# Gathers of source ids and edge keys moved from the setup into the rows' stage, and the stage before layer 1 dissolved into layer 1's first tiles

## The chip, the cores and the metric

The kernel runs on one NeuronCore of a Trainium2 chip. The metric is device time in microseconds (us) of one execution; lower is better. The core has five engines that run in order, each with its own queue, and that wait for one another through semaphores: PE (TensorE, matrix products and transposes), DVE (VectorE), ACT (ScalarE), POOL (GpSimd, which also issues the indirect DMAs) and SP (SyncE, which here only issues DMAs).

## The reference

One layer of a graph network with attention over 6250 nodes of 256 features and 200,000 edges (dst is sorted).

```
xn = layernorm(x)
A  = normalized adjacency with self loops: norm(e) = dinv[src]*dinv[dst], dinv = 1/sqrt(degree)
gnn = relu(A (relu(A (xn W1) + b1) W2) + b2)
q, k, v = split(xn W_qkv + b_qkv); q, k minus their row mean; q2 = q*q, k2 = k*k
k2 = l2norm_over_nodes(k2 / (rowsum(k2) + 1e-7)); q2 = l2norm_over_columns(q2 / (rowsum(q2) + 1e-7))
mix = (v + q2 (k2^T v) / sqrt(N)) W_mo + b_mo
x1 = x + gnn + mix
out = x1 + slice_attention(layernorm(x1))      (64 slices, 8 heads)
```

## The kernel before, in words

The nodes are cut into T = 49 tiles of 128 rows. The program is a sequence of stages; each is a block in which every engine has its own list of work, and a block ends with a barrier of all engines. The stages around the change are:

1. **The setup.** It finds where each run of dst begins, counts degrees, prepares weights, and makes the edge keys. A window is two nodes; there are G = 7 groups of 112 partitions with WPS = 4 windows each, so 28 gathers. POOL issues 28 indirect DMAs (L307), each of which brings 128 source ids for each of 112 windows. DVE splits all ids at once into a low part (L425, L426) and a tile number (L428 to L431), over 3584 elements per partition. PE transposes the 56 blocks (L488) and ACT copies them as 14 groups into key_lo and key_hi (L516). SP stores the degrees to DRAM and loads them back turned (L271, L273); PE turns them, DVE copies them to degT (L434) and computes the flag (L437). A branch on that flag (`nc.values_load`, `nc.If(general == 1)`) follows; it isn't taken with these inputs.
2. **A block for dinv:** ACT takes a root (L616), DVE a reciprocal and two scalings (L621 to L624).
3. **The rows' stage.** It runs over 49 tiles with rings of 4 buffers. In its iteration t, PE does project(t) (L772 and four passes of L774), turn(t+1) (two transposes, L763) and gather(t-2) (k2 sums L782, then two transposes of q2, L789). DVE does norm(t+1) (L699 to L706), stats(t+2) (L691, L694), over_norm(t-2) (L731 to L737), over_sums(t-1) (L721 to L725) and halves(t+1) (L711). ACT does norms(t-2), std(t+2), keep(t+1), squares(t) and turned(t-3). POOL adds one tile (L821). SP loads x and stores the turned tiles.
4. **The stage between** (L886 and on). kx, the sums that the rows' stage leaves in PSUM, is copied (L918) and turned (L966), multiplied by wvo (L972) and scaled to mkv (L954, L958). Beside it runs a chain that finds the largest entries: two DVE reductions (L919, L920), an ACT square (L907), a partition_all_reduce on POOL (L903), an ACT root (L911) and eight DVE steps (L931 to L948), which give the scales of layer 1.
5. A second `nc.If(general == 1)`, whose body (sum_edges) is long and isn't run.
6. **Layer 1.** POOL writes two iotas (L1238, L1239). DVE makes one-hot matrices from the keys (hots, L1277) in 8 batches per tile, with a ring of 4 batches. PE multiplies them into adjacency blocks (build, L1321, 64 per tile), ACT copies these to `at` (store, L1379), POOL adds the self loops (L1249), and PE aggregates (L1332). Tile t+1 is built while tile t is aggregated. The iteration t = -1 only builds. relu(t-1) on ACT uses the scale dsc.

## Time and profile before

| what | us |
|---|---|
| timed executions (3) | 2064.79, 2066.60, 2067.97; median 2066.6 |
| span of the profiled execution | 2066.3 |
| PE busy | 1886.4 (91%) |
| DVE busy | 1177.8 (57%) |
| ACT busy | 850.7 (41%) |
| POOL busy | 301.8 (15%) |

The profiled execution's own time is its span, 2066.3 us. The busy shares are means over stages with different limits: from layer 1 on PE is full, while in the first sixth of the span the limit changes from stage to stage. So the parts below are read by stage, from the timeline (start, duration, engine, line, operation) and from windows of time.

### The profile page before, as it was taken

What the parts mean: (1) busy time and instruction counts of PE and PEld (TensorE: products, weight loads), DVE (VectorE), ACT (ScalarE), POOL (GpSimd) and SP (SyncE); (2) the same over time, 40 slices, a digit from 0 to 9 for tenths busy, and PEclk for the clock granted to TensorE, in tenths of its full rate; (3) what the DMA queues carried; (4) which work ended last, traced back from release to release, by engine and by line L of the source; (5) the groups of instructions that cost most, each with busy time, mean ns of one, the idle gap of its engine ahead of it and who ended that gap; (6) DMA issues with size and microseconds to landing.
All of it is one profiled execution on the core that took longest, in us unless ns stands there. A gap on an engine that the chain in (4) does not pass through costs nothing. (4 is left out here: it accounts for less than half of the span.)

```text
span 2066.3 us, 45220 instructions
## 1 busy us (share of the span) xinstructions
PE 1886.4 (91%) x18840; PEld 1417.3 (69%) x18840; DVE 1177.8 (57%) x2715; ACT 850.7 (41%) x1948; POOL 301.8 (15%) x418
## 2 busy tenths in 40 slices
PE   3069994999999999999979999999999999999598
PEld 3035552555555555555549999999999999999476
DVE  6369985666666666666623555555555555555322
ACT  2157772665656666566531222232222322322100
POOL 3502121000000000000020111111111111111033
PEclk7569996999999999999999999999999999999699
DMA  3113331232222223232335444444444444442087
GB/s 95 32 36 112 113 106 42 95 126 101 119 109 111 117 103 125 95 125 94 126 115 184 145 144 141 141 141 141 141 141 141 141 144 145 144 144 96 13 265 233
DMA packets 92701, 252.13 MB, mean 122 GB/s; under 512 B 14142, under 2 KB 59346, under 8 KB 79938
## 3 DMA queue, kind: packets, MB, share of 16 engines
q1 hardware_dynamic: 69225, 218.83, 29.7%
q10 hardware_dynamic: 21096, 25.65, 3.5%
q0 software_dynamic: 2176, 4.75, 0.9%
q8 instruction: 150, 2.46, 0.5%
q14 instruction: 54, 0.44, 0.1%
HBM read 131.99 MB, written 118.02 MB: 121 GB/s over the span
## 5 line engine op out<-in xcount | busy, mean ns | idle before, releaser
L1332 PE MATMUL ps<-hs,at 128*128 128x512 f16 x2401 | 667.8, 378 | 3.3 <-POOL at L1249 3.3
L1530 PE MATMUL ps<-at,big 128*128 128x128 f16 x9604 | 577.0, 219 | 6.5 <-DMA at<-at_scratch 6.5
L1530 PEld LDWEIGHTS ps<-at,big 128*128 128x128 f16 x9604 | 556.0, 98 | 34.2 <-issue 8.0
L1379 ACT CAST at<-ps 128x392 f16<-128x392 f32 x784 | 375.3, 486 | 302.3 <-PE ps L1321 286.2
L1321 PE MATMUL ps<-big 128*128 128x98 f16 x3136 | 472.3, 209 | 15.2 <-DVE big L1277 15.2
L1321 PEld LDWEIGHTS ps<-big 128*128 128x128 f16 x3136 | 298.3, 98 | 149.9 <-issue 14.8
L1332 PEld LDWEIGHTS ps<-hs,at 128*128 128x128 f16 x2401 | 229.8, 97 | 151.7 <-POOL at L1249 3.5
L1277 DVE TENSOR_TENSOR big<-big,key_lo 128x1024 f16<-128x1024 f16 x392 | 268.4, 685 | 0.0
L1277 DVE TENSOR_TENSOR big<-big,key_hi 128x784 f16<-128x784 f16 x392 | 219.1, 559 | 15.4 <-POOL big L1239 10.4
L1644 DVE SCALAR_TENSOR_TENSOR big<-ps,small,blogb 128x512 f32<-128x512 f32 x49 | 36.8, 751 | 230.9 <-PE ps L1566 230.9
L1747 POOL TENSOR_TENSOR key_lo<-key_lo,big 128x512 f32<-128x512 f32 (+1 forms) x49 | 61.9, 1263 | 706.6 <-ACT big L1705 706.6
L1288 DVE TENSOR_TENSOR big<-ps,big 128x256 f32<-128x256 f32 x49 | 20.8, 425 | 201.6 <-ACT big L1387 201.6
L1249 POOL TENSOR_TENSOR at<-at,ident 128x120 f16<-128x120 f16 x98 | 31.9, 336 | 655.5 <-ACT at L1379 655.5
L1693 ACT ACTIVATE big<-big,eps 128x1 f32<-128x1 f32 x49 | 14.5, 296 | 224.2 <-DVE big L1629 224.2
L1695 ACT CAST big<-ps 128x512 f16<-128x512 f32 x49 | 28.7, 585 | 170.9 <-PE ps L1557 170.9
L774 PE MATMUL ps<-at,big 128*128 128x512 f32 (+1 forms) x196 | 98.6, 626 | 0.0
L1022 PE MATMUL ps<-hs 128*128 128x256 f32 (+1 forms) x392 | 90.7, 391 | 8.6 <-DMA hs<-x_scratch 8.4
L1022 PEld LDWEIGHTS ps<-hs 128*128 128x128 f32 (+1 forms) x392 | 75.0, 195 | 24.6 <-DMA hs<-x_scratch 14.2
L1697 ACT ACTIVATE big<-big 128x512 f32<-128x512 f32 x49 | 30.8, 629 | 146.9 <-DVE big L1650 146.9
L488 PE MATMUL ps<-ident,big 112*128 112x112 f32 x56 | 10.3, 373 | 88.7 <-DVE big L426 84.3
L1615 DVE SCALAR_TENSOR_TENSOR big<-ps,dun,key_hi 128x256 f32<-128x256 f32 x49 | 23.7, 484 | 106.5 <-PE ps L1539 106.5
L1582 PE MATMUL ps<-big 128*128 128x256 f16 (+1 forms) x588 | 74.5, 278 | 0.0
(273 smaller groups left out, 2334.9 us busy)
## 6 DMA issues: line engine op xcount, KB each, us to landing
at_scratch<-at SPq DMA_DIRECT2D x49, 1568.0 KB, 5.2
at<-at_scratch SPq DMA_DIRECT2D x49, 1568.0 KB, 6.9
xT_scratch<-big SPq DMA_DIRECT2D x98, 128.0 KB, 2.0
big<-xT_scratch SPq DMA_DIRECT2D x49, 256.0 KB, 3.1
wT_scratch<-big ACTq DMA_DIRECT2D x49, 256.0 KB, 2.0
hs<-wT_scratch SPq DMA_DIRECT2D x49, 256.0 KB, 3.4
big<-in_x_dram SPq DMA_DIRECT2D x96, 128.0 KB, 2.3
x_scratch<-big ACTq DMA_DIRECT2D x48, 128.0 KB, 1.7
```

The costliest lines, as they stand in the source:

```text
L774: mm = te.matmul(ps[0:rows(t), 1 + b % 2, :], lhsT=xt_now[:, b, c, 0:rows(t)], rhs=wqk[:, c, :], start=False, stop=(c == CB - 1))
L1022: mm = nc.tensor.matmul(ps[0:rows(t), b, 0:C], lhsT=turned_in[:, b, i * NT:i * NT + rows(t)], rhs=w, start=(i == 0), stop=(i == len(weight ...
L1249: g.tensor_tensor(block_t, block_t, ident16[:, cols], ALU.add).then_inc(looped, 1)
L1277: last = v.tensor_tensor(hot[:, s, :].rearrange("p (q k r) -> p q k r", k=width, r=2), iota.rearrange("p (o k) r -> p o k r", o=1).to_broa ...
L1321: te.matmul(ps[:, BANKS[i // UW % len(BANKS)], i % UW * KC:(i % UW + 1) * KC], lhsT=hot_lo[:, s, :].rearrange("p (q k r) -> p q k r", k=P, ...
L1332: mm = te.matmul(ps[:, 2 + b, :], lhsT=at[:, b, k * P:(k + 1) * P], rhs=hs[:, k, :], start=(k == 0), stop=(k == T - 1))
L1379: a.copy(to.rearrange("p k (i j) -> p k i j", j=WIN), ps[:, BANKS[m % len(BANKS)], 0:UW * KC].rearrange("p (i k j) -> p k i j", i=UW, j=WI ...
L1530: mm = te.matmul(ps[:, b, c * NT:(c + 1) * NT], lhsT=hs2[:, k, h * C + c * P:h * C + (c + 1) * P], rhs=at[:, b, k * P:(k + 1) * P], start= ...
L1582: mm = te.matmul(ps[:, 6 + p // 2, (p % 2) * C:(p % 2 + 1) * C], lhsT=w_half[0:rows(t), b, p * P:(p + 1) * P], rhs=x_half[0:rows(t), b, :] ...
L1644: v.scalar_tensor_tensor(out=lg[0:NT, b].rearrange("p h d -> p (h d)"), in0=ps[0:NT, 4, :], scalar=unscale[0:NT], in1=blogb[0:NT, :], op0= ...
L1697: a.activation(ew[0:NT, b], lg[0:NT, b], ACT.Exp).then_inc(exp_ready, 1)
L1747: g.tensor_tensor(w_acc[:, :, 0:rows(t)], w_acc[:, :, 0:rows(t)], wt[:, b, :, 0:rows(t)], ALU.add).then_inc(w_added, 1)
```

## The change

- **Setup.** The 28 source gathers, the key arithmetic, the 56 key transposes and the 14 ACT copies are taken out. What stays is one comparison over 3584 elements (`second`). The two iotas of layer 1 come in on POOL (the low one from base 0).
- **dinv's block** is merged into the rows' stage: ACT's root comes first on ACT, DVE's reciprocal and scalings before the first stats.
- **Rows' stage.** POOL issues one source gather in each of tiles 0 to 27, ahead of its addition. DVE makes the keys of one group (512 elements per partition, five instructions) at the end of iterations 10, 14, ... 34. ACT casts the low keys (one copy of 512 in iterations 11, 15, ... 35) and stores 224 columns in each of 28 iterations. PE turns two blocks of keys ahead of the xn transposes of tiles 13 to 40, into the free half of the same bank.
- **The stage between** is gone. kx's copy, transposes, product and the scaling to mkv go into layer 1's iteration -1. The chain of scales goes into iterations 0 and 1; partition_all_reduce is replaced by a PE transpose, a DVE reduction over two rows and a PE product. relu(0) waits for the scales.

The lines of DVE's scales(), halves_of_weights() and column_norms() and those of multiply_kx() and turn_kx() are those of the removed stage, with other semaphores. PE's 56 transposes (L488) and ACT's 14 copies (L516) of the setup are removed as well.

```
+                nc.gpsimd.iota(iota_hi, [[1, KC], [0, 2]], base=0, channel_multiplier=0,
+                               allow_small_or_imprecise_dtypes=True)
+                nc.gpsimd.iota(iota_lo, [[1, P], [0, 2]], base=0, channel_multiplier=0,
+                               allow_small_or_imprecise_dtypes=True)
...
-                pool.wait_ge(cut_ready, 1)
-                pool.wait_ge(src_padded, 32)
-                for n in range(G * WPS):
-                    pool.indirect_dma_start(
-                        out=srcg[:, n, :], out_offset=None, in_=src_dram.rearrange("(e a) -> e a", a=1),
-                        in_offset=bass.IndirectOffsetOnAxis(ap=wlo[:, n // WPS, n % WPS:n % WPS + 1], axis=0)
-                    ).then_inc(src_gathered, 16)
-                pool.wait_ge(src_gathered, 16 * G * WPS)
...
-                step(v.tensor_tensor(held, slots, over(many.rearrange("p g w -> p (g w)")), ALU.is_lt))
-                step(v.tensor_copy(some, pairs[:, :, :, 0]))
-                dve.wait_ge(src_gathered, 16 * G * WPS)
-                step(v.tensor_scalar(src_lo, srcg, P - 1, None, ALU.bitwise_and))
-                v.scalar_tensor_tensor(out=keyl, in0=src_lo, scalar=1.0, in1=held, op0=ALU.add, op1=ALU.mult
-                                       ).then_inc(keys_made, 1)
-                step(v.tensor_scalar(tile_of, srcg, 7, None, ALU.logical_shift_right))
-                dve.wait_ge(keys_made, 1)
-                step(v.tensor_tensor(held, slots, over(some.rearrange("p g w -> p (g w)")), ALU.is_ge))
-                v.scalar_tensor_tensor(out=keyh, in0=tile_of, scalar=float(WIN), in1=held, op0=ALU.mult, op1=ALU.add
-                                       ).then_inc(keys_made, 1)
+                step(v.tensor_copy(first, pairs[:, :, :, 0]))
+                v.tensor_tensor(second.rearrange("p g w s -> p (g w) s"),
+                                slot.rearrange("p (o s) -> p o s", o=1).to_broadcast([GW, G * WPS, CAP]),
+                                first.rearrange("p g (w o) -> p (g w) o", o=1).to_broadcast([GW, G * WPS, CAP]), ALU.is_ge)
...
+                dve.wait_ge(deg_root, 1)
+                v.reciprocal(dinv[:, :], dinv[:, :]).then_inc(dinv_ready, 1)
+                dve.wait_ge(dinv_ready, 1)
+                v.tensor_scalar(dsc[:, :], dinv[:, :], SH, None, ALU.mult)
+                v.tensor_scalar(dun[:, :], dinv[:, :], 1.0 / SH, None, ALU.mult).then_inc(dinv_ready, 1)
+                dve.wait_ge(dinv_ready, 2)
+                def edge_keys(g):
+                    r = g % 2
+                    dve.wait_ge(gathered[g % 3], before_sources[g % 3] + 16 * WPS * (g // 3 + 1))
+                    if g >= 2:
+                        dve.wait_ge(keyl_ready, g - 1)
+                        dve.wait_ge(xn_turned, KEYS_TURN + WPS * (g - 2) + WPS)
+                    v.tensor_scalar(src_lo[:, r], srcg[:, g], P - 1, None, ALU.bitwise_and).then_inc(parts_made, 1)
+                    v.tensor_tensor(beyond, slot.rearrange("p (o s) -> p o s", o=1).to_broadcast([GW, WPS, CAP]),
+                                    many[:, g].rearrange("p (w o) -> p w o", o=1).to_broadcast([GW, WPS, CAP]), ALU.is_ge
+                                    ).then_inc(parts_made, 1)
+                    dve.wait_ge(parts_made, 4 * g + 2)
+                    v.tensor_scalar(srcg[:, g], srcg[:, g], 7, None, ALU.logical_shift_right).then_inc(parts_made, 1)
+                    v.scalar_tensor_tensor(out=second[:, g], in0=beyond, scalar=1024.0, in1=second[:, g],
+                                           op0=ALU.mult, op1=ALU.add).then_inc(parts_made, 1)
+                    dve.wait_ge(parts_made, 4 * g + 4)
+                    v.scalar_tensor_tensor(out=keyh[:, r], in0=srcg[:, g], scalar=float(WIN), in1=second[:, g],
+                                           op0=ALU.mult, op1=ALU.add).then_inc(keys_made, 1)
...
+                    if reached(t, KEYS_LAG) and (t - KEYS_LAG) % WPS == 0 and (t - KEYS_LAG) // WPS < G:
+                        edge_keys((t - KEYS_LAG) // WPS)
...
+                def turn_keys(n, bank):
+                    g, high, pair = n // WPS, n % WPS // 2, n % 2
+                    if high:
+                        pe.wait_ge(keys_made, g + 1)
+                    else:
+                        pe.wait_ge(keyl_ready, g + 1)
+                    for j in range(2):
+                        te.transpose(ps[:, bank, C + j * GW:C + (j + 1) * GW],
+                                     (keyh if high else keyl)[:, g % 2, 2 * pair + j, :], ident[0:GW, 0:GW])
                 def turn(t, b):
                     pe.wait_ge(xn_ready, t + 1)
                     if reached(t, 2):
                         pe.wait_ge(xnT_stored, t - 1)
+                    if reached(t, KEYS_TURN + 2):
+                        pe.wait_ge(keys_stored, min(t - KEYS_TURN - 1, KEY_PARTS))
+                    if reached(t, KEYS_TURN) and within(t, KEYS_TURN + KEY_PARTS):
+                        turn_keys(t - KEYS_TURN, 3 * (b % 2))
...
+                def gather_sources(g, j):
+                    pool.indirect_dma_start(
+                        out=srcg[:, g, j, :], out_offset=None, in_=src_dram.rearrange("(e a) -> e a", a=1),
+                        in_offset=bass.IndirectOffsetOnAxis(ap=wlo[:, g, j:j + 1], axis=0)).then_inc(gathered[g % 3], 16)
+                pool.wait_ge(src_padded, 32)
                 def tile(t, b, u):
+                    if t < WPS * G:
+                        if t % WPS == 0 and t // WPS >= 3:
+                            pool.wait_ge(parts_made, 4 * (t // WPS - 3) + 1)
+                        gather_sources(t // WPS, t % WPS)
...
+                a.activation(dinv[:, :], degT[:, :], ACT.Sqrt, bias=ones[:, 0:1]).then_inc(deg_root, 1)
+                def low_keys(g):
+                    act.wait_ge(parts_made, 4 * g + 1)
+                    if g >= 2:
+                        act.wait_ge(xn_turned, KEYS_TURN + WPS * (g - 2) + 2)
+                    a.copy(keyl[:, g % 2], src_lo[:, g % 2]).then_inc(keyl_ready, 1)
+                def store_keys(t, b):
+                    n = t - KEYS_TURN
+                    g, high, pair = n // WPS, n % WPS // 2, n % 2
+                    a.copy((key_hi if high else key_lo)[:, g * GW * WPS:(g + 1) * GW * WPS]
+                           .rearrange("p (w j) -> p j w", j=WPS)[:, 2 * pair:2 * pair + 2],
+                           ps[:, 3 * (b % 2), C:C + 2 * GW].rearrange("p (j w) -> p j w", w=GW)).then_inc(keys_stored, 1)
                 def tile(t, b, u):
+                    if reached(t, KEYS_LAG + 1) and (t - KEYS_LAG - 1) % WPS == 0 and (t - KEYS_LAG - 1) // WPS < G:
+                        low_keys((t - KEYS_LAG - 1) // WPS)
...
+                    if reached(t, KEYS_TURN - 1) and within(t, KEYS_TURN - 1 + KEY_PARTS):
+                        store_keys(t + 1, (b + 1) % RING)
...
-            @block.gpsimd
-            def _(pool):
-                pool.wait_ge(split_step, 2)
-                nc.gpsimd.partition_all_reduce(small[:, 11:13], small[:, 9:11], P, RMAX).then_inc(split_step, 1)
...
+                def widest():
+                    v.tensor_reduce(small[:, 13:14], b1b[:, :], AX.X, ALU.max, apply_absolute_value=True)
+                    v.tensor_reduce(small[:, 9:10], wlog_f, AX.X, ALU.max, apply_absolute_value=True).then_inc(scale_step, 1)
...
+                        if t == -1 and i == 3:
+                            column_norms()
+                        if t == -1 and i == 6:
+                            weights_of_q2()
+                        if t == 0 and i == 0:
+                            widest()
+                        if t == 0 and i == 6:
+                            widest_of_all()
+                        if t == 1 and i == 0:
+                            dve.wait_ge(scale_step, 6)
+                            v.tensor_copy(small[:, 11:13], peak_row).then_inc(scale_step, 1)
+                        if t == 1 and i == 3:
+                            scales()
+                        if t == 1 and i == 5:
+                            halves_of_weights()
+                v.tensor_copy(kx, ps[:, 4:6, 0:C + 3]).then_inc(kx_kept, 1)
...
+                        if t == -1 and i == 7:
+                            turn_kx()
+                        if t == -1 and i == 31:
+                            multiply_kx()
+                        if t == 0 and i == 20:
+                            turn_peaks()
+                        if t == 0 and i == 60:
+                            spread_peaks()
+                        if t == 1 and i == 63:
+                            pe.wait_ge(scale_step, 7)
...
+                    if t == 0:
+                        act.wait_ge(scale_step, 12)
...
+                        if t == -1 and m == 2:
+                            act.wait_ge(kx_turned, 1)
+                            a.copy(kxT.rearrange("p a b c -> p (a b c)"), ps[:, 2, :]).then_inc(kxT_kept, 1)
+                            a.activation(rn, kx[:, :, C + 2], ACT.Sqrt).then_inc(rn_step, 1)
+                        if t == 0 and m == 0:
+                            a.activation(square, w1[:, :, :].rearrange("p a b -> p (a b)"), ACT.Square,
+                                         accum_out=small[:, 10:11]).then_inc(scale_step, 1)
+                        if t == 1 and m == 2:
+                            act.wait_ge(scale_step, 7)
+                            a.activation(small[:, 15:16], small[:, 12:13], ACT.Sqrt, scale=float(C * P)).then_inc(scale_step, 1)
...
```

## Rows read from the trace of the kernel before

**Rows 1.** Windows: start:end, length, busy (instructions) per engine, granted clock, DMA share, GB/s
```profile
180.00:200.00 20.00, 20.00 (x76) 11.28 (x74) 18.34 (x82) 15.41 (x62) 4.35 (x6) 1.00 0.37 118
300.00:312.00 12.00, 10.90 (x40) 5.92 (x38) 8.05 (x35) 8.38 (x35) 2.48 (x4) 1.00 0.25 83
318.00:326.00 8.00, 1.25 (x5) 0.85 (x5) 3.43 (x9) 1.02 (x4) 0.37 (x1) 0.50 0.00 0
500.00:700.00 200.00, 200.00 (x1628) 118.53 (x1627) 129.21 (x245) 119.85 (x273) 16.52 (x42) 1.00 0.27 114
```

**Rows 2.** Timeline, end of the setup: start, us, engine, line, operation, idle before
```profile
63.14 3.88 DVE L422 TENSOR_TENSOR big<-big 112x3584 f32<-112x3584 f32 x1
63.47 4.36 POOL L307 DMA_INDIRECT big<-src_scratch,big  x1 [23.52 <-issue]
64.57 0.30 SPq L273 DMA_DIRECT2D big<-deg_scratch  x1
68.14 0.93 POOL L307 DMA_INDIRECT big<-src_scratch,big  x1 [0.31 <-issue]
...
102.89 2.14 DVE L425 TENSOR_SCALAR big<-big 112x3584 int32<-112x3584 int32 x1 [35.65 <-DMA big<-src_scratch,big]
105.06 3.89 DVE L426 SCALAR_TENSOR_TENSOR big<-big 112x3584 f32<-112x3584 int32 x1
...
110.12 7.18 ACT L516 CAST key_lo<-ps 128x448 f16<-128x448 f32 x7 [48.23 <-PE ps L488]
...
124.11 0.14 DVE L437 TENSOR_SCALAR flag<-ps 1x1 int32<-1x1 f32 x1
```

**Rows 3.** Timeline, dinv's block and the first tile of the rows' stage
```profile
127.93 1.28 ACT L616 ACT_TABLE_LOAD   x1 [0.93 <-PEq L167]
...
130.20 0.18 DVE L624 TENSOR_SCALAR dun<-dinv 128x49 f32<-128x49 f32 x1
...
132.70 0.43 DVE L691 BATCH_NORM_STATS2 big<-big 128x6 f32<-128x256 f32 x1 [1.91 <-DMA big<-in_x_dram]
```

**Rows 4.** Timeline, one tile of the rows' stage in its steady run
```profile
161.25 0.38 PE L772 MATMUL ps<-at 3*128 3x512 bf16 x1
...
162.85 0.72 POOL L821 TENSOR_TENSOR big<-big 128x256 f32<-128x256 f32 x1 [2.82 <-ACT big L858]
...
163.23 0.36 DVE L735 TENSOR_TENSOR big<-big 128x1 f32<-128x1 f32 x1
...
163.63 0.35 DVE L737 TENSOR_SCALAR big<-big 128x256 f32<-128x256 f32 x1
...
164.48 0.38 PE L789 MATMUL ps<-ident,big 128*128 128x128 f32 x2
...
164.79 0.38 PE L772 MATMUL ps<-at 3*128 3x512 bf16 x1
```

**Rows 5.** Timeline of DVE, an early tile of the same stage
```profile
145.38 0.16 DVE L735 TENSOR_TENSOR big<-big 128x1 f32<-128x1 f32 x1
145.57 0.81 DVE L737 TENSOR_SCALAR big<-big 128x256 f32<-128x256 f32 x1
```

**Rows 6.** Timeline, the stage between and the start of layer 1
```profile
318.15 0.70 DVE L918 COPY big<-ps 128x518 f32<-128x518 f32 x1 [3.09 <-PEq L629]
...
325.87 3.78 PE L972 MATMUL ps<-wvo,big 128*128 128x256 f32 x8 [5.84 <-DVE big L928]
...
330.60 0.61 DVE L958 TENSOR_SCALAR mkv<-big 128x256 f32<-128x256 f32 x2
338.90 1.20 POOL L1238 IOTA big<- 128x196 f16 x1 [14.62 <-issue]
...
341.62 0.57 DVE L1277 TENSOR_TENSOR big<-big,key_hi 128x784 f16<-128x784 f16 x1 [10.40 <-POOL big L1239]
...
351.51 3.58 POOL L1249 TENSOR_TENSOR at<-at,ident 128x120 f16<-128x120 f16 x2 [9.93 <-ACT at L1379]
...
355.15 0.61 PE L1332 MATMUL ps<-hs,at 128*128 128x512 f16 x1 [3.33 <-POOL at L1249]
```

256 lines of the change are left out of this document (119 added, 137 removed).

## The prediction

> **What bounds the kernel now.** I read the busy shares by slices first, then windows, then the timeline at the joints between stages. From layer 1 on PE is busy 200.00 of 200.00 us at full clock while DVE is busy 129.21 [rows 1]; nothing that the change touches lies there except layer 1's first two iterations. The time to be won lies before, where stages follow one another in series.
>
> In the setup, DVE waits 35.65 us for the 28 gathers, and the chain from the first gather to the flag is POOL, DVE, PE, ACT one after another until 124.25 [rows 2]. The rows' stage is different: PE is busy 20.00 of 20.00 us and DVE 18.34 [rows 1]. A tile takes 164.79 - 161.25 = 3.54 us [rows 4]. I read the missing 8% of DVE as the gaps between its 13 instructions and not as room, because DVE has no listed wait there. Its only room is in L735: it takes 0.36 us and ends at 163.59, just as POOL's addition (until 163.57) does [rows 4], and takes 0.16 us when POOL is idle [rows 5]. So DVE alone would need about 3.54 - 0.20 = 3.34 us a tile. PE and DVE are both close to being the bound, and this decides what moved work costs there.
>
> **The change part by part.**
>
> *End of the setup: minus 56.6.* What remains after 63.14 is the comparison over 3584 elements, priced by L422 at 3.88 us, which ends near 67.3 after its small copy. The load of the degrees is issued at 64.57; if it lands after about 2 us, as the load of x does, it is hidden behind that comparison [rows 2, 3]. Copy and flag add 0.3: the end is 67.6 instead of 124.25, a gain of 56.6. The two iotas take 2.7 us on POOL (338.90 to 341.62 [rows 6]). They move to the very start, where POOL's next step waits for DVE's row index anyway; they cost nothing, and 2.7 if that wait were gone.
>
> *dinv merged: minus 2.2.* DVE's last scaling ends at 130.38 and the first stats start at 132.70, after the load of x [rows 3]. In one block SP issues the load when ACT loads its table (127.93), and the 2 us load is hidden behind root and scalings. Stats start at about 130.5.
>
> *Keys in the rows' stage: plus 18.* For one group, five DVE instructions over 512 elements, a seventh of 3584: two like L425 (2.14 / 7 = 0.31) and three like L426 (3.89 / 7 = 0.56) [rows 2]; together 2.3, and 5 x 0.06 for starts and semaphore steps: 2.6 us. On PE, two transposes a tile: L789's two of 128 columns keep PE for 0.31 until the next product [rows 4]; for two of 112 columns, in a run of four, I take 0.25. On ACT, 224 columns are half of L516's 7.18 / 7 = 1.03 [rows 2], 0.5 us a tile, and a cast of 512 elements a group, 0.6 to 0.7 as L918 [rows 6]; ACT is busy 15.41 of 20.00 [rows 1], that is 2.7 us of 3.54, so 3.4 with them.
>
> Four tiles took 14.16 us. PE alone would need 4 x (3.54 + 0.25) = 15.2; DVE alone 4 x 3.34 + 2.6 = 16.0. Those two are bounds (7 groups: plus 7 and plus 13), and they hold only if an engine could run far ahead. It can't: over_norm(t-2), L737, ends at 163.98, and PE wants it at 164.48 [rows 4], a lead of 0.5. After a group's keys DVE is 2.6 late, PE waits about 2.6 - 0.5 - 0.2 (no hold by POOL then) - 0.2 (its own key transposes ran in the wait) = 1.7, and in the other three tiles DVE can't build up a lead, because L731 waits for ACT's norms, which come behind squares and now behind the key store. So a group costs 15.2 + 1.7 - 14.16 = 2.7, seven 19. Where the lead is partly regained it is nearer DVE's bound. I take 18, ends 6 and 24.
>
> *Gathers in the rows' stage: plus 1.* One is 0.93 us on POOL plus 0.31 ahead of it [rows 2]; POOL is idle 2.82 us of each tile [rows 4]. Behind a gather on POOL stands only L821, whose result ACT needs three tiles later. The first gather of the setup took 4.36, ending 0.8 after DVE's 3.88 us comparison [rows 2]: POOL was held while DVE ran it. In the rows' stage DVE's instructions are below 0.5 us and small ones lie between, so I expect 1 to 1.5 us per gather, which fits. The other way, POOL holds DVE: L737 took 0.81 instead of 0.35 beside L821 [rows 5]. A gather may do that at each of 28 tiles: 0 to 28 x 0.46 = 13. [...]
>
> The Trainium skill (GPSIMD Engine Reference, Specifications and Key points) says that GpSimd shares its SBUF interfaces with VectorE and contends with instructions in a two-port mode or with two SBUF inputs. By that rule nearly every 256-column DVE instruction here is in the way of a gather; the trace's 4.36 against 0.93 agrees, and it is the second rival below.
>
> *The stage between and layer 1's entry: minus 14.* Before, the stage began at 318.15, ended at 331.21, and POOL's iota began 338.90 [rows 6]: 7.7 us of barrier and branch, which I keep. DVE's first hots came at 341.62. Now: 318.0 + 7.7 = 325.7, kx's copy 0.7 [rows 6], hots at 326.4, 15.2 earlier. Into iteration -1 come three column norms (small ones of 0.16 [rows 5] with their waits, 0.6), four instructions for mkv (two took 0.61, two more read PSUM at L918's rate, together 1.5), and on PE the product of eight passes, 3.78 [rows 6] at a granted clock of 0.50 [rows 1], and four transposes of half that width (1.0). PE reaches that product with batch 3 of 8 and DVE wants it after batch 6; I reckon 1 us of waiting. So 3.1 of the 15.2 are given back. Next, in iteration -1 POOL's self loops took 3.58 for two additions, until DVE's back-to-back hots had filled the ring, and PE waited 3.33 for them [rows 6]. Now two reductions (1280 elements with one input; at L918's 518 in 0.70 that is 1.7 us) stand after the first batch of iteration 0, and POOL gets in between: 2.9 earlier. In iterations 0 and 1, DVE takes on 1.7 and about 4 us. It is busy 129.21 of 200.00 us in this layer [rows 1], so a third of a tile is free; but the order makes single batches of hots late, so plus 1. Sum: -15.2 + 3.1 - 2.9 + 1 = -14. If POOL stays held and the reductions stand ahead of it, -9; if PE's clock rises in iteration -1, -17.
>
> The Trainium skill (VectorE: DVE Perf Modes, the perf-mode tier table) has tensor_reduce at the plain mode only. That rule would leave the interface to POOL and give the -2.9; without it the time would be 2.9 later. The trace of before has no POOL work beside a long reduction.
>
> **Sum.** -56.6 - 2.2 + 18 + 1 - 14 = -53.8. On the profiled span of 2066.3 that is 2012.5; the median of the timed runs lies 0.3 above the span, so 2013.
>
> **The rivals.**
>
> 1. *The keys are hidden better.* DVE's waits are looser than I read and only PE's transposes count: plus 6 instead of plus 18, so 2001, down to 1997 with the best entry. For it: ACT has 4.6 of 20 us free. Against: DVE 18.34 of 20.00 [rows 1].
> 2. *Gathers and DVE obstruct each other.* Each gather takes 3 us and more as the first did, or holds a DVE instruction for 0.46. With 3.4 a gather, POOL's tile becomes 3.4 + 0.31 + 0.72 = 4.4 against 3.54: 28 x 0.9 = 25, of which some 8 lie behind the keys' own delay; or 13 on DVE. With it 2025 to 2038. For it rows 2 and 5; against, DVE's short instructions.
> 3. *The entry wins less.* Branch or instruction supply costs more now, or the waits in iterations 0 and 1 stop PE: plus 5 to 9, so 2018 to 2022.
> 4. *Slower: PE's clock falls in the rows' stage.* PE now pauses 1.7 us in every fourth tile. At the lower level (1.2 instead of 2.4 GHz) a tile in which PE is always busy takes up to twice 3.54 = 7.1, against the forecast's 3.54 + 18/28 = 4.2, so 2.9 more. Over 28 tiles that is 81: 2094. It decides against the change from 54 / 2.9 = 19 tiles at the lower level on. For it: in the stage between, with little work for PE, the granted clock was 0.50. Against: with 1.1 us of pauses in 12 it stayed at 1.00 [rows 1].
> 5. *The change doesn't do what it says*: another wait ends the setup late. Nothing after 67.6 remains in it, 2 in 100.
>
> **How the numbers follow.** Forecast (2003 to 2024, rival 3 within it for the most part) 72 in 100; rival 1 below 2003 8; rival 2 above 2024 15; rival 4 3; rival 5 2. From 2001 to 2030 holds 80 in 100: it leaves out half of rival 1, more than half of rival 2, and 4 and 5. A measurement of this kernel can tell a change from about 0.2% (4 us). All cases but 4 and part of 5 are faster by more: faster 0.96, same 0.01, slower 0.03.
>
> **What would show it.** Flag at 67 to 68 us; first stats 6.2 to 6.4 us after it; the rows' stage from first stats to its end some 19 us longer than before, with tiles 11, 15, ... 35 (DVE's keys at their head) near 5.5 us and their neighbours near 3.8; POOL's gathers 1 to 1.5 us; the gap to layer 1 near 7.7; from kx's copy to the first aggregate about 14.5. The forecast is wrong if tiles 0 to 9 of the rows' stage are longer than 3.6 (gathers in the way), if the granted clock in the stage is below 1.00, or if the gap before layer 1 differs.

## The result, and the profile after

The changed kernel takes 2013.8 us, the median of four timed runs (2009.7 to 2019.06); the kernel before, beside it, 2067.06 (2064.79 to 2067.97). The ratio is 0.9742, with a 95% interval of 0.9724 to 0.976. The forecast was 2013. The sum was right and three of its terms were not: they cancelled.

The profiled execution of the changed kernel is its longest, 2019.06, with a span of 2017.1. So the traces differ by 2066.3 - 2017.1 = 49.2 us, where the medians differ by 53.3. All steps below are differences between the two traces and add up to 49.2.

| stretch (first stats, last ScalarE copy of the rows' stage, first hots, first aggregate, first gather of layer 1, end) | before | after | difference | forecast |
|---|---|---|---|---|
| start to first stats | 132.70 | 72.34 | -60.4 | -58.8 |
| rows' stage, to the end of its last copy | 183.2 | 217.3 | +34.1 | +19 |
| to the first hots | 25.7 | 3.1 | -22.6 | |
| to the first aggregate | 13.5 | 12.5 | -1.1 | -14 for these four |
| to the first gather of layer 1 (372.07, now 324.08) | 16.9 | 18.9 | +2.0 | |
| from there to the end | | | -1.2 | |

The timeline after, end of the setup and start of the rows' stage (start, us, engine, line, operation, idle before):

```profile
64.46 3.89 DVE L417 TENSOR_TENSOR big<-big 112x3584 f32<-112x3584 f32 x1
65.69 0.30 SPq L275 DMA_DIRECT2D big<-deg_scratch  x1
67.50 0.31 PE L470 MATMUL ps<-ident,big 49*128 49x49 f32 x1 [42.03 <-DMA big<-deg_scratch]
68.39 0.13 DVE L424 TENSOR_SCALAR flag<-ps 1x1 int32<-1x1 f32 x1
69.44 1.28 ACT L892 ACT_TABLE_LOAD   x1 [6.44 <-PEq L174]
...
72.34 0.43 DVE L687 BATCH_NORM_STATS2 big<-big 128x6 f32<-128x256 f32 x1 [0.38 <-DMA big<-in_x_dram]
```

The setup now ends with the comparison and the flag, as forecast, at 68.5. The next stage begins 0.9 us after it. Before, 3.7 us lay between the flag and the table load [rows 2, 3]. I had kept them as a cost of the branch. They were not: ScalarE was still storing keys.

The timeline of ScalarE before, around the flag:

```profile
119.85 7.15 ACT L516 CAST key_hi<-ps 128x448 f16<-128x448 f32 x7 [2.55 <-PE ps L488]
```

Its last copy ends at 127.00, 2.8 us after the flag, and 0.93 before the table load.

Now the rows' stage. DVE and PE after, around the keys of the first group:

```profile
118.11 0.41 DVE L673 TENSOR_SCALAR big<-big 112x512 int32<-112x512 int32 x1
118.44 0.68 DVE L674 TENSOR_TENSOR big<-big 112x512 f32<-112x512 f32 x1
119.16 0.43 DVE L678 TENSOR_SCALAR big<-big 112x512 int32<-112x512 int32 x1
119.50 0.69 DVE L679 SCALAR_TENSOR_TENSOR big<-big 112x512 f32<-112x512 f32 x1
120.22 0.69 DVE L682 SCALAR_TENSOR_TENSOR big<-big 112x512 f32<-112x512 int32 x1
120.83 0.15 DVE L695 RECIPROCAL big<-big 128x1 f32<-128x1 f32 x1
...
121.70 0.44 PE L776 MATMUL ps<-ident,big 128*128 128x128 f32 x2 [1.58 <-DVE big L699]
...
123.46 0.69 PE L802 MATMUL ps<-ident,big 128*128 128x128 f32 x2 [0.45 <-DVE big L733]
...
124.61 3.78 PE L787 MATMUL ps<-at,big 128*128 128x512 f32 x4
```

DVE's five key instructions keep it from 118.11 to 120.83, 2.7 us. The next norm is late by that, and PE waits 1.58 + 0.45 us. Then the four passes of the projection, 1.98 us at 118.13, take 3.78. The windows (start:end, length, busy and instructions of PE, PEld, DVE, ACT and POOL, granted clock, DMA share, GB/s) say why:

```profile
114.00:117.00 3.00, 3.00 (x12) 1.58 (x11) 2.78 (x13) 2.23 (x10) 1.12 (x3) 1.00 0.44 128
...
120.00:123.00 3.00, 1.42 (x7) 0.85 (x6) 2.78 (x11) 0.69 (x3) 2.03 (x2) 1.00 0.22 74
123.00:126.00 3.00, 2.55 (x6) 1.23 (x6) 2.75 (x13) 2.31 (x11) 0.62 (x1) 0.54 0.22 68
126.00:129.00 3.00, 3.00 (x8) 1.38 (x7) 1.74 (x8) 0.26 (x1) 1.04 (x2) 0.50 0.41 109
129.00:132.00 3.00, 3.00 (x11) 1.84 (x11) 1.25 (x6) 2.74 (x11) 0.00 (x0) 0.82 0.02 6
```

After the pause the granted clock falls from 1.00 to 0.50, that is from 2.4 to 1.2 GHz, and is back 6.8 us later. The starts of the projection give the length of each tile. Before, the 28 tiles that now carry keys took 3.54 us each, 99.1 together. They now take 130.2, in groups of four of 20.4, 17.1, 20.5, 17.1, 20.5, 17.2 and 17.4: the clock falls in the first, third and fifth group and not in the others. The falls of the third and fifth come after a single long pause of 1.88 us; in the four groups without a fall it is 1.50 to 1.75, and 0.26 about 1.7 us later. Tiles 2 to 9, which carry a gather and no keys, still take 3.54. The first two take 5.20 and 5.21 (4.66 and 2.98 before). There too it is the clock: it is at 0.50 until 85.7, 13.4 us after the first stats, where before it rose 6.7 us after them.

The joint to layer 1 after:

```profile
289.26 0.37 ACT L889 COPY big<-ps 128x256 f32<-128x256 f32 x1 [1.19 <-PE ps L802]
...
292.06 0.70 DVE L1339 COPY big<-ps 128x518 f32<-128x518 f32 x1 [3.30 <-PEq L582]
292.68 0.56 DVE L1293 TENSOR_TENSOR big<-iota_hi,key_hi 128x784 f16<-128x784 f16 x1
...
297.67 1.96 PE L1370 MATMUL ps<-wvo,big 128*128 128x256 f32 x8
304.41 0.59 POOL L1209 TENSOR_TENSOR at<-at,ident 128x120 f16<-128x120 f16 x2 [15.79 <-ACT at L1448]
305.14 0.59 PE L1392 MATMUL ps<-hs,at 128*128 128x512 f16 x1 [0.27 <-POOL at L1209]
```

From the stage's last copy to the copy of kx it is 2.4 us, not the 2.2 + 7.7 that I had kept from before [rows 6]. POOL's self loops take 0.59 instead of 3.58, and PE waits 0.27 for them instead of 3.33. The product with wvo runs at full clock, in 1.96 instead of 3.78.

### The profile page after: what moved, and what is told of

It reads as the page before. It is cut to its first block and busy times, and to the rows that moved or that the text cites. A ratio compares the mean times of both kernels' runs of the same rounds, so it can differ in the third digit from the quotient of the medians.

```text
span 2017.1 us, 45282 instructions
## 1 busy us (share of the span) xinstructions
PE 1894.1 (94%) x18843; PEld 1415.6 (70%) x18843; DVE 1185.0 (59%) x2748; ACT 852.7 (42%) x1970; POOL 300.0 (15%) x417
## 5 line engine op out<-in xcount | busy, mean ns | idle before, releaser
L1293 DVE TENSOR_TENSOR big<-iota_lo,key_lo 128x1024 f16<-128x1024 f16 x392 | 268.2, 684 | 0.0
L1293 DVE TENSOR_TENSOR big<-iota_hi,key_hi 128x784 f16<-128x784 f16 x392 | 218.9, 559 | 1.1 <-PE ps L1353 1.0
L787 PE MATMUL ps<-at,big 128*128 128x512 f32 (+1 forms) x196 | 106.2, 667 | 0.0
L1647 PE MATMUL ps<-wlog,big 128*128 128x512 f16 x294 | 72.7, 384 | 0.7 <-ACT big L1776 0.7
```

The costliest lines, as they stand in the source:

```text
L787: mm = te.matmul(ps[0:rows(t), 1 + b % 2, :], lhsT=xt_now[:, b, c, 0:rows(t)], rhs=wqk[:, c, :], start=False, stop=(c == CB - 1))
L1293: last = v.tensor_tensor(hot[:, s, :].rearrange("p (q k r) -> p q k r", k=width, r=2), iota.rearrange("p (o k) r -> p o k r", o=1).to_broa ...
L1647: mm = te.matmul(ps[0:NT, 4, :], lhsT=xn2T[:, b, xh, c * NT:(c + 1) * NT], rhs=wlog16[:, wh, c, :], start=(c == 0 and xh == wh == 0), stop ...
```

## The experiments

Eleven kernels ran. Each line of results gives the median, the range, and the ratio to the kernel before on the same chip with its interval. Code is cut and shortened to what is changed. The first four kernels ran on one chip, the next four on a second, the last three on a third, and the kernel before took 2066.3, 2065.0 and 2069.1 us there. So a difference between the medians of two kernels from different chips is uncertain by up to 4 us; the stretches of the traces are the firmer evidence.

**The all-reduce out of the kernel before.** What made the 7.7 us before layer 1?

```diff
-                nc.gpsimd.partition_all_reduce(small[:, 11:13], small[:, 9:11], P, RMAX)
+                te.transpose(ps[0:2, 2, 0:P], small[:, 9:11], ident[:, :])
+                v.tensor_reduce(peak[:, 0:1], ps[0:2, 2, 0:P], AX.X, ALU.max)
+                v.tensor_scalar(peak[:, 2:4], ident[0:2, 0:2], peak[:, 0:1], None, ALU.mult)
+                te.matmul(ps[:, 3, 0:2], lhsT=ones_row, rhs=peak[:, 2:4], start=True, stop=True)
+                v.tensor_copy(small[:, 11:13], ps[:, 3, 0:2])
```

> The kernel before with one thing changed: the largest entries are brought together by a PE transpose, a DVE reduction and a PE product instead of partition_all_reduce on POOL. Theory A (what POOL does around that instruction is what made 7.7 us pass between the stage between and layer 1): the gap from the last DVE instruction of that stage (mkv) to POOL's first iota falls from 7.7 to about 1 us, and the stage itself is 3 to 5 us shorter, so 10 to 12 us less in all, near 2055. Theory B (barrier, branch and instruction supply make the gap, as the prediction had it): the gap stays at 7.7 and only the stage's 3 to 5 us are won, near 2062.

2059.3 us (2056.6 to 2060.6), ratio 0.9961 [0.9948, 0.9975]; 7 us less than the kernel before. Its timeline at the joint:

```profile
329.89 0.62 DVE L963 TENSOR_SCALAR mkv<-big 128x256 f32<-128x256 f32 x2
331.32 1.21 POOL L1247 IOTA big<- 128x196 f16 x1 [14.96 <-POOLq L889]
...
334.03 0.57 DVE L1286 TENSOR_TENSOR big<-big,key_hi 128x784 f16<-128x784 f16 x1 [3.52 <-POOL big L1248]
```

The iota starts 0.8 us after mkv is done, where it started 7.7 after. Barrier and branch are still there, so the gap came with the all-reduce. That it was POOL's change back to an ordinary instruction fits, but was not tested apart. From the copy of kx (319.59) to mkv the stage is 2.1 us shorter, 10.9 instead of 13.1, where 3 to 5 were expected. From the last ScalarE copy to the first hots the trace has 16.7 us instead of 25.7: 9.0 are won at the joint, against the 10 to 12 of theory A. The median shows 7; the rows' stage of the traced execution was 1.9 longer than before.

**An unused all-reduce at the end of the rows' stage, in the kernel after.**

```diff
                 pipeline(tile, T, RING)
+                pool.wait_ge(k4_added, T)
+                nc.gpsimd.partition_all_reduce(small[:, 3:4], small[:, 2:3], P, RMAX)
```

> The changed kernel with one partition_all_reduce put back on POOL at the end of the rows' stage, its result unused. Theory A: layer 1's first DVE instruction comes some 14 us later against the rows' end than in the changed kernel (2.4 us from the last ACT copy to kx's copy become 16 or so), total near 2028. Theory B: only the instruction itself delays the barrier, 4 us at most, total near 2018.

One run, 2016.2 us; span 2014.2.

```profile
282.63 0.72 POOL L846 TENSOR_TENSOR big<-big 106x256 f32<-106x256 f32 x1 [1.77 <-ACT big L885]
284.21 0.37 ACT L891 COPY big<-ps 128x256 f32<-128x256 f32 x1 [1.40 <-PE ps L802]
289.07 0.38 POOL L850 PARTITION_ALL_REDUCE small<-small  x1 [5.72 <-issue]
292.28 0.70 DVE L1341 COPY big<-ps 128x518 f32<-128x518 f32 x1 [8.78 <-PEq L582]
```

The all-reduce has everything it needs at 283.35 and starts 5.72 us later. From the last ScalarE copy (284.58) to the copy of kx it is now 7.7 us instead of 2.4: 5.3 more. Neither theory had this number: A wanted some 14 and a total near 2028, B 4 at most. The way back to ordinary instructions can't be seen here, since POOL's next instruction is wanted only 12 us later. In the kernel before, the all-reduce started (323.91) 3.6 us after its last input and 5.8 after the first instruction of its stage (318.13). The profile writes 0.38 us for an instruction that costs 5.7 ahead of it, and up to 6.9 (7.7 - 0.8) behind it.

The Trainium skill (GPSIMD Engine Reference, 2.1 Instruction dispatch) states that the first call of a freshly loaded kernel of that engine pays about 6 us for loading its code, without an instruction in the profile. The 5.72 us agree with it; that it is code which is loaded no run here shows.

Up to its last tile this kernel's rows' stage is that of the kernel after, so it shows the stage a second time:

```profile
121.25 0.44 PE L776 MATMUL ps<-ident,big 128*128 128x128 f32 x2 [1.58 <-DVE big L699]
...
123.01 0.44 PE L802 MATMUL ps<-ident,big 128*128 128x128 f32 x2 [0.45 <-DVE big L733]
```

```profile
121.00:124.00 3.00, 2.30 (x10) 1.44 (x11) 2.75 (x14) 1.82 (x8) 0.98 (x2) 1.00 0.09 19
124.00:127.00 3.00, 3.00 (x14) 1.79 (x12) 2.71 (x15) 1.99 (x9) 1.66 (x2) 1.00 0.40 134
```

The same two pauses, 1.58 and 0.45 us, and this time the clock stays at 1.00. It falls in the third group (for 3.4 us) and in the seventh (for 6.8); the 28 tiles take 125.8 us where they took 130.2. So a pause of this length makes a fall possible and not certain, and which group it meets changes from execution to execution.

**The two long reductions later.** Does POOL get in because they stand ahead of it?

```diff
-                        if t == 0 and i == 0:
+                        if t == 0 and i == 4:
                             widest()
```

> The changed kernel with the two reductions over single inputs (widest) moved from behind batch 0 of iteration 0 to behind batch 4, so that four batches of hots stand back to back when POOL wants to add the first self loops. Theory interface (DVE's two-input instructions hold POOL): the 120-column addition takes about 3.4 us again instead of 0.4, and the first aggregate comes 2.5 to 3.3 us later against kx's copy (16 instead of 13.1). Rival (the addition was slow for another reason): it stays at 0.4 and the first aggregate does not move by more than 0.3.

One run, 2017.7 us.

```profile
302.29 3.73 POOL L1209 TENSOR_TENSOR at<-at,ident 128x120 f16<-128x120 f16 x2 [15.80 <-ACT at L1448]
306.17 0.59 PE L1392 MATMUL ps<-hs,at 128*128 128x512 f16 x1 [3.41 <-POOL at L1209]
```

The self loops are held again, 3.73 us, and the first aggregate comes 16.2 us after the copy of kx (289.95) instead of 13.1. The forecast's -2.9 for this is shown. This kernel's rows' stage too is that of the kernel after: its clock falls in the same three groups (130.3 us for the 28 tiles), and at the start of the stage it rises 7.7 us after the first stats instead of 13.4, and there the first two tiles take 8.1 us instead of 10.4. At the first gather of layer 1 only 1.7 of the 3.1 us are left (33.8 us after the copy of kx against 32.0).

**DVE's five key instructions spread over four iterations.** The burst is what differs; the work is the same.

```diff
-                    if reached(t, KEYS_LAG) and (t - KEYS_LAG) % WPS == 0 and (t - KEYS_LAG) // WPS < G:
-                        edge_keys((t - KEYS_LAG) // WPS)
+                    if reached(t, KEYS_LAG) and (t - KEYS_LAG) // WPS < G:
+                        edge_keys((t - KEYS_LAG) // WPS, (t - KEYS_LAG) % WPS)   # part 0: and, shift; 1: is_ge; 2: second; 3: keyh
```

> The changed kernel with the five DVE key instructions of a group spread over four iterations (two small ones, then one in each) instead of standing in a row. Theory burst (the row of five makes DVE 2.7 us late at once, PE pauses for it, and in every second group the granted clock falls after the pause): no tile above 4.3 us, four tiles of a group in 16.0 to 16.4 instead of 17.1 or 20.5, granted clock 1.00 throughout the key tiles; 7 groups save 7 x 0.9 + 3 x 3.3 = 16 us, near 1998. Rival (ACT's key stores or PE's key transposes bound the stage): tiles of 3.74 and the group's sum stay, no more than 3 us less.

2004.3 us (2002.1 to 2005.3), ratio 0.9698 [0.9685, 0.9712]: 9.5 us below the kernel after. The 28 tiles take 117.0 instead of 130.2, a group 16.8, and the granted clock is 1.00 from 80 to 260 us. I had expected 16.0 to 16.4 a group and a run near 1998. A window in the middle of the tiles with keys:

```profile
110.00:140.00 30.00, 28.35 (x110) 15.29 (x108) 27.85 (x110) 22.83 (x87) 12.70 (x16) 1.00 0.38 115
```

PE, which was full before [rows 1], now has 1.65 us of waits in 30, and DVE is busy 93% of the time, with no more gaps than the small ones between its instructions: it is the bound now.

**PE kept busy in its pause, in the kernel after.** If the clock falls because PE pauses, unused products in the pause must keep it up, though DVE's burst stays.

```diff
+                    if reached(t, KEYS_LAG + 1) and (t - KEYS_LAG - 1) % WPS == 0 and (t - KEYS_LAG - 1) // WPS < G:
+                        pe.wait_ge(sq_ready, 2 * t)
+                        for _ in range(4):
+                            te.matmul(ps[:, 1 + (b + 1) % 2, C:2 * C], lhsT=wqk[:, 0, 0:P], rhs=wqk[:, 0, 0:C],
+                                      start=True, stop=True)
                     if within(t, T - 1):
                         turn(t + 1, (b + 1) % RING)
```

> The kernel after, with TensorE given four f32 products of 128x256 (some 1.7 us at full clock, results unused) in the seven iterations in which it waits for VectorE's burst of five key instructions; VectorE's burst stays. Theory A (of the 34 us that the rows' stage became longer, some 10 to 13 are the clock, which is granted at .50 for some 6 us after every second pause of TensorE; the pause is what brings it down): the granted clock stays 1.00 from 80 to 290 us, the groups of four tiles that took 20.5 us take some 17.2, and the run takes 2001 to 2007. Rival B (the longer groups are VectorE's own work piling up, and the low clock only falls into a time in which TensorE would wait anyway): the clock may stay up, but the time stays within 2011 to 2019; and if the filler delays TensorE, it is longer by up to 7 x 1.7 = 12 us.

2006.9 us (2003.9 to 2007.9), ratio 0.9715 [0.9698, 0.9731]: 6.9 below the kernel after, with more work. The windows behind the first pause:

```profile
121.00:124.00 3.00, 3.00 (x12) 1.60 (x13) 2.71 (x14) 2.09 (x9) 0.95 (x2) 1.00 0.29 94
124.00:127.00 3.00, 3.00 (x12) 1.66 (x11) 2.78 (x13) 2.87 (x11) 0.71 (x1) 1.00 0.25 79
```

The clock stays at 1.00 and all groups take 17.2 to 17.5, 121.8 in all: 8.5 less than in the kernel after. By the ratios, each to the kernel before on its own chip, it is 5.6 below the kernel after. So the low clock is a cost of its own and not time in which PE would wait anyway. The spread kernel is another 4.8 us shorter in these tiles: that is what the burst costs beyond the clock (and what the filler may cost).

**The gathers alone.** The kernel after without the making of keys: DVE's instructions, ScalarE's copies and PE's transposes.

```diff
-                        edge_keys((t - KEYS_LAG) // WPS)
-                        turn_keys(t - KEYS_TURN, 3 * (b % 2))
-                        low_keys((t - KEYS_LAG - 1) // WPS)
-                        store_keys(t + 1, (b + 1) % RING)
+                g.memset(key_lo[:, :], 0.0)
+                g.memset(key_hi[:, :], 0.0)
```

> The kernel after, without the making of the keys in the rows' stage: VectorE's five instructions of a group, ScalarE's copy of the low keys, TensorE's key transposes and ScalarE's key stores are left out, and the key tables are set to zero by GpSimd, so that layers 1 and 2 compute with other edges; the 28 source gathers stay in the rows' stage. Theory A (the gathers cost the rows' stage nothing, all 34 us are the key work): tiles of 3.54 us throughout, first statistics to last ScalarE copy within 2 us of the kernel before's 183.2, and the run takes 2013.8 - 34 = 1978 to 1983. Rival B (each gather holds something for a part of its 0.93 us, hidden so far by TensorE being the bound): tiles with a gather take 3.6 to 4.0 and the stage is 3 to 12 us longer, run 1983 to 1992.

1985.9 us (1985.8 to 1985.9), ratio 0.9618 [0.9602, 0.9634]. The 28 tiles that would carry keys take 99.2, as before, and tiles 2 to 9 take 3.54: a gather costs nothing. The rows' stage, first stats to last ScalarE copy, takes 183.8 us (183.2 before). The run's time lies 3 us above the range of theory A and in that of rival B, but no tile is longer, as B would have it. GpSimd's two memsets, which I had added, delay the first stats from 72.34 to 74.96, and that is 2.6 of them.

**The comparison with the number of edges on GpSimd.** From the spread kernel; two of DVE's five instructions go, GpSimd gets three.

```diff
-                        v.tensor_tensor(beyond, slots, many_of_g, ALU.is_ge)
-                        v.scalar_tensor_tensor(out=second[:, g], in0=beyond, scalar=1024.0, in1=second[:, g], ...)
+                        g.tensor_tensor(beyond, slots, many_of_n, ALU.subtract)          # tile 4n
+                        g.tensor_scalar(beyond, beyond, 0.0, 128.0, ALU.max, ALU.mult)   # tile 4n + 1
+                        g.tensor_tensor(second[:, n], second[:, n], beyond, ALU.add)     # tile 4n + 2
```

> The kernel with the key work spread over four iterations, and further: the comparison of the slots with the number of edges and its addition to the high key (two of VectorE's five instructions, 1.37 us of 2.9 a group) are made by GpSimd in three instructions (a difference, a bound with a scale, a sum) one an iteration, four or more iterations ahead of their use. Theory A (with the work spread, a tile lasts as long as VectorE's 3.25 us plus its share of the key work, unless TensorE's 3.54 + 0.20 is more): the tile with keys falls from 4.19 on average to 3.74 to 3.85, the rows' stage gets 8 to 11 us shorter than in the spread kernel, run 1993 to 1996. Rival B (VectorE and GpSimd slow each other down: GpSimd's instructions of 112x512 hold VectorE's, or are held and delay its sum of each tile): tiles of 3.9 to 4.3, run 1998 to 2006.

2029.2 us (2024.3 to 2031.2), ratio 0.9824 [0.9805, 0.9842]: 25 us slower than the spread kernel, and far above the ranges of both theories. Its DVE and POOL:

```profile
139.92 0.35 DVE L720 TENSOR_SCALAR big<-big 128x256 f32<-128x256 f32 x1
...
143.59 1.54 DVE L720 TENSOR_SCALAR big<-big 128x256 f32<-128x256 f32 x1
143.90 1.06 POOL L841 TENSOR_TENSOR big<-big 112x512 f32<-112x512 f32 x1
```

L720 takes 0.35 us where POOL is idle. At 143.59 it takes 1.54 and ends at 145.13, after POOL's subtraction (until 144.96). Work moved from DVE to GpSimd came back to DVE as longer instructions. The 28 tiles take 131.9, and the tiles ahead of them up to 6.0. A part of this is the clock again, which is at 0.50 for 3.4 us in three places (from 95.4, 116.0 and 139.8 us).

The Trainium skill (SBUF — State Buffer, SBUF: two separate sides) states that the port pair which VectorE and GpSimd share is locked for a whole instruction, against VectorE's instructions in a two-port mode or with two SBUF inputs, and that the engine which comes second blocks. These rows agree that one blocks: 1.54 us for an instruction of 0.35 beside one of 1.06. Which engine had the lock they don't show, since by the rows VectorE's began first, by 0.31 us.

**Two small edits on top of it.** Layer 1's iotas behind the row gathers, and unused products in layer 1's first iteration.

```diff
                 pool.wait_ge(row_gathered, 16 * G)
+                nc.gpsimd.iota(iota_hi, ...)
+                nc.gpsimd.iota(iota_lo, ...).then_inc(iotas_ready, 1)
...
+                        if t == -1 and i in (47, 55, 63):
+                            for _ in range(4 if i == 55 else 1):
+                                te.matmul(ps[:, 5, C:2 * C], lhsT=wvo[:, 0, 0:P], rhs=wvo[:, 0, :], start=True, stop=True)
```

> The kernel with the comparisons on GpSimd, and two edits more: GpSimd's two index patterns of layer 1 are made after the row gathers, where VectorE waits for these, and no longer beside VectorE's comparisons at 5 us; and TensorE gets six unused f32 products of 128x256 between the last batches of layer 1's first iteration, where it waits for VectorE. Theory A: the setup is 1.0 us shorter (VectorE's comparison goes back from 13.69 to 12.66 us), and the granted clock stays at 1.00 through the first aggregation instead of falling to .50 for 6 us, worth 2 to 4 us: run 3 to 5 us below the kernel with the comparisons on GpSimd alone. Rival B (the start of the aggregation is bound by VectorE's batches, not by TensorE's clock; the patterns hold the gathers or the row counts at their new place): difference 0 to 1 us either way.

2027.2 us (2024.5 to 2033.4), ratio 0.9814 [0.9797, 0.983]. The medians differ by 2.0 and the ranges overlap, so the run decides nothing. Two of its stretches point to theory A: the flag at 65.83 instead of 67.95, and from the copy of kx to the first gather of layer 1 29.8 instead of 30.7. In the second the clock stays at 1.00, where in the kernel without the products it was at 0.50 for 3.4 us.

> The kernel with the key work spread over four iterations on VectorE, and the two edits tried before on top of the slower kernel: layer 1's two index patterns after the row gathers, and six unused f32 products on TensorE between the last batches of layer 1's first iteration. Theory A (both edits are worth here what their stretches showed there: the flag 2.1 us earlier, the way from the copy of the column sums to the first gather of layer 1 0.9 us shorter): 2004.3 - 2.1 - 0.9 = 2000 to 2002.5. Rival B (the gain at the flag is taken back by the rows' start, as the 0.2 us lower median of the slower kernel might say): 2003 to 2005.

The same two edits on the spread kernel: 1999.9 us (1995.8 to 2000.7), ratio 0.966 [0.9641, 0.9678], slightly below the expected 2000. The windows at layer 1's first aggregate, of the spread kernel and then of this one:

```profile
284.00:287.00 3.00, 0.73 (x12) 0.42 (x9) 2.96 (x8) 2.07 (x6) 0.00 (x0) 1.00 0.01 3
287.00:290.00 3.00, 2.11 (x14) 1.21 (x15) 3.00 (x6) 1.01 (x3) 0.59 (x2) 0.54 0.16 67
290.00:293.00 3.00, 3.00 (x16) 1.57 (x15) 3.00 (x7) 1.45 (x4) 0.00 (x0) 0.50 0.96 401
```

```profile
285.00:288.00 3.00, 3.00 (x33) 2.68 (x32) 2.96 (x8) 2.43 (x6) 0.00 (x0) 1.00 0.01 3
288.00:291.00 3.00, 2.44 (x24) 1.66 (x23) 3.00 (x6) 1.25 (x3) 0.59 (x2) 1.00 0.16 67
291.00:294.00 3.00, 3.00 (x29) 1.69 (x28) 3.00 (x6) 2.28 (x7) 0.00 (x0) 1.00 0.96 401
```

The clock stays up, and the first gather comes 29.8 us after the copy of kx instead of 31.7. The flag is at 66.68 instead of 67.84. The kernel with the unused all-reduce tells the clock's part from that of the products: it has no products, its clock happened to stay up at the first aggregate, and it too needs 29.8 us.

**The comparison left out.** The spread kernel without the two instructions that went to GpSimd above, and with no other engine doing them.

> The kernel with the key work spread, but with the comparison of the slots with the number of edges and its addition to the high key left out altogether (two of VectorE's five instructions, given to no other engine); slots beyond a window's edges keep the keys of their neighbours' edges, so the layers compute with other edges. It is the kernel with the comparisons on GpSimd without GpSimd's three instructions. Theory A (with spread work a tile lasts as long as the busier of VectorE's 3.25 us plus its key work and TensorE's 3.74; GpSimd's instructions alone made that kernel 25 us slower by holding VectorE's): tiles with keys 3.74 to 3.9, run 1993 to 1997. Rival B (a part of the slowdown is in the order of the work: three instructions in two iterations, the shift and the high key one iteration after each other, make TensorE wait): tiles of 4.2 and more in one iteration of four as before, run 2000 to 2005.

1994.6 us (1993.9 to 1996.7), ratio 0.9639 [0.9623, 0.9655]. The 28 tiles take 109.6. Three of four take 3.74 us, which is PE's 3.54 and its key transposes; one takes 4.2 to 4.5. So theory A holds for most tiles, and 0.7 us a group stay with the order, as rival B had it. The kernel with the comparison on GpSimd is 2029.2 - 1994.6 = 34.7 us slower. Not all of it is GpSimd's. The two ran on different chips. In the traces 2.7 us lie in the first two tiles, whose length goes with the clock. The three places with a low clock make some 5 us, an estimate from the 3.3 us of one twice as long. And its order is not quite the same: it makes the high keys one iteration after the shift and not three, and its last two groups, with GpSimd's instructions all done, still take 16.3 instead of 15.5, some 5 us over seven groups. By these estimates some 20 us are left for GpSimd.

**The comparisons in f16**, on top of the late iotas and the filler. Slots, first counts and edge counts are multiples of 128 in f16, broadcast in pairs; a difference and a maximum take the place of the comparison and the sum.

```diff
-                v.tensor_tensor(second, slot (f32), first (f32), ALU.is_ge)             # 3584 columns, setup
+                v.tensor_tensor(second, slot (f16), first2 (f16, pairs), ALU.is_ge)
-                        v.tensor_tensor(beyond, slot, many, ALU.is_ge); v.scalar_tensor_tensor(second = beyond * 1024 + second)
+                        v.tensor_tensor(beyond, slot, many2, ALU.subtract); v.tensor_tensor(second, second, beyond, ALU.max)
```

> The kernel with spread keys, late patterns and filler, and VectorE's comparisons in f16 instead of f32: the one over all slots at the end of the setup (3.89 us for 3584 columns), and the two of a group in the rows' stage (0.68 and 0.69 us for 512 columns), these as a difference and a maximum. Theory A (VectorE runs f16 operands in pairs at about 0.6 ns a column, as layer 1's comparison of 1024 columns in 0.68 us shows): 3.89 becomes some 2.1, 0.68 becomes some 0.4: setup 1.8 us shorter, VectorE's key work 2.6 to 2.1 us a group, worth 2 to 4 us over seven groups: run 3.5 to 6 us below the same kernel in f32. Rival B (the broadcast operand or the maximum runs at one column a cycle in f16 as well): difference within 1 us.

1993.3 us (1992.0 to 1996.4), ratio 0.9637 [0.9619, 0.9655]: the best version, 6.6 us below the same kernel in f32 on the same chip, a little more than the 3.5 to 6 expected, and 20 below the kernel after.

```profile
62.32 2.02 DVE L423 TENSOR_TENSOR big<-big 112x3584 f16<-112x3584 f16 x1
65.56 0.21 DVE L427 COPY degT<-ps 128x49 f32<-128x49 f32 x1 [1.22 <-PE ps L476]
...
165.27 0.42 DVE L684 TENSOR_TENSOR big<-big 112x512 f16<-112x512 f16 x1
```

2.02 us for 3.89, 0.42 for 0.68. In the setup only 1.0 of the 1.9 us is won, since DVE now waits 1.22 for the turned degrees. The 28 tiles take 111.2 instead of 117.0, 5.8 less where 2 to 4 were expected. In the traces the first two tiles are 2.2 shorter as well, where the clock rose sooner; that is not the edit's.

## Why the prediction was right, and where it was not

*End of the setup and dinv, -58.8; measured -60.4.* The mechanism was right. Two things were missed. The flag did not end the setup before: ScalarE's stores did, until 127.00, so the branch cost 0.9 us and not 3.7, and the first stats come 3.9 us after the flag instead of the forecast's 6.2 to 6.4. Against that, the iotas were not free. "They cost nothing" failed at the start of the setup: DVE's cast of 15 elements, 0.18 us before, takes 1.12 beside them (below), and the comparison over 3584 elements starts at 64.46 where it started at 63.14. With the iotas moved away the cast takes 0.17 again.

*Keys in the rows' stage, +18; measured +34.1 for the stage, +31.1 in the 28 tiles with keys.* This is the step that failed, in size and in one mechanism. The prediction's own sign of being wrong, a granted clock below 1.00 in the stage, came up. The parts, from the sums of the 28 tiles: 99.1 without keys; 117.0 with the keys spread (+17.9); 121.8 in a burst with the clock held up (+22.7); 130.2 in a burst as written (+31.1). PE's transposes took 0.20 a tile, 5.6 in all, where I had 0.25. In the groups without a fall of the clock the burst costs 2.2 to 2.4 us on top of the transposes (17.15 to 17.4, less 14.16 and 0.8), where I had 1.7. That the keys cost 17.9 when spread is no support for my 18, which was reckoned for a burst. What is left is mostly the clock. I had the clock only as a rival that turns the change into a loss, at 81 us and 3 in 100, as if it stayed low in all 28 tiles. It came in small coin: 3 of 7 groups at 3.3 us each (20.4 against 17.1), 10 us together. "With 1.1 us of pauses in 12 it stayed at 1.00" was my evidence against; a pause of 1.88 us, or 1.58 and 0.45 close together, brought it down in some places and left it up in others. The first two tiles are 2.8 longer. In the thirteen kernels of this document this pair takes 7.6 to 10.4 us, whatever was edited later in the stage, and its length follows the moment at which the clock rises: 7.6 to 7.8 where that is some 7 us after the first stats, 10.4 where it is 13. So these 2.8 are the clock too, and not the keys.

*Gathers, +1; measured 0.* Tiles with a gather and no keys take 3.54, and leaving all key work out gives the stage of before. No run shows anything for which the forecast's 1 us could stand; 28 gathers slow no tile. Rival 2 was wrong about the gathers, and right that the two engines can hold each other: GpSimd arithmetic in the same place made the kernel 34.7 us slower, some 20 of them by that, as estimated above.

*The stage between and layer 1's entry, -14; measured -22.9 in this trace.* The step that failed is "7.7 us of barrier and branch, which I keep". It was the price of partition_all_reduce, which the change removes, and this was in the diff. Another of the prediction's signs of being wrong, a different gap before layer 1, stood here. Out of the kernel before alone it is worth 7 us. The rest held in its direction: the self loops are released (-2.9; -3.1 at the first aggregate), and the product with wvo ran at the full clock, the case for which I had -17. From the first aggregate to the first gather 2.0 us are given back where I had 1. That is the clock, which is at 0.50 for 6.8 us there: with it up, in the kernel with the unused all-reduce, this stretch takes 16.7 us, as before (16.9), and not 18.9. Keeping it up there, together with the earlier flag, is worth 3.1 us in these two stretches and 4.4 by the medians of two kernels, from two chips.

*The sum.* The rows' stage is 15 longer than forecast. The entry gives 9 more than forecast, the setup 1.6 more. 15.1 - 8.9 - 1.6 is 4.6, and by so much the trace's difference of 49.2 is short of the forecast's 53.8. The median is 53.3 because the profiled execution is the longest of four that lie 9 us apart. A part of this scatter is the clock's: the same rows' stage was traced three times, with 3, 3 and 2 falls, and took 217.3, 214.9 and 212.7 us. It is not all, since the kernel before, whose clock does not fall in these tiles, scatters by up to 8 us on one chip. The right time was partly luck: two errors of 15 and 9 us with opposite signs. Each term has to be checked against its own stretch.

## What to carry to other kernels

When work is moved into a stage where the matrix engine is full and its feeder nearly so, ask how long the matrix engine will pause at a time, not only how much work is added: the same keys cost 2.6 us a group spread over four iterations, 3.2 in one burst, and 4.4 with the falls of the clock after the pauses (3.8 in another execution). A gap between stages is not a barrier's price until the last instruction on every engine has been looked at, and GpSimd's kind of instruction on both sides. Moving element work to GpSimd beside a busy VectorE can cost more than it takes away; a cheaper type on VectorE gave what the move did not.

## What the runs showed of the hardware

- GpSimd's partition_all_reduce is drawn as 0.37 us. At the end of the rows' stage it started 5.72 us after all it needed was there, and in the kernel before an iota behind it came 7.7 us after the stage's end instead of 0.8.
- Pauses of TensorE of 1.5 to 1.9 us every 17 us or so brought the granted clock from 1.00 to 0.50 for 3.4 or 6.8 us in three, three and two of seven like places, in three traces of the same stage. The same pair of pauses, 1.58 and 0.45, was followed by a fall in one trace and not in another. A fall of 6.8 us cost 3.3.
- With unused f32 products in the pause it stayed at 1.00 in all seven places (one trace), and at layer 1's first aggregate in all three traces with products there; of the eight traces of the new entry without them one has no fall.
- An iota on GpSimd holds even a small VectorE instruction. The timeline of the cast at the start of the kernel before, then of both in the kernel after:

```profile
4.16 0.18 DVE L335 CAST big<-big 110x15 f32<-110x15 int32 x1 [2.87 <-DMA big<-in_dst_dram]
```

```profile
3.58 1.49 POOL L293 IOTA iota_lo<- 128x256 f16 x1
...
4.25 1.12 DVE L333 CAST big<-big 110x15 f32<-110x15 int32 x1 [2.82 <-DMA big<-in_dst_dram]
```

- An indirect gather of 112 rows of 128 words takes 0.93 us on GpSimd and slows none of the tiles of 3.54 us in which it runs; beside VectorE's comparison of 3.88 us it took 4.36 [rows 2].
- VectorE's comparison of 3584 columns takes 3.89 us in f32 and 2.02 in f16 with the broadcast operand laid out in pairs; for 512 columns it is 0.68 and 0.42.
